# A decoder layer on one core: the spectral stage with one forward transform of the context, exponentials with bias on ScalarE and both products of the weights on GpSimd, one slot deeper

## The reference, cut to what matters

```python
corr = jnp.fft.ifft(qf * jnp.conj(kf), axis=2).real
w, idx = jax.lax.top_k(corr.transpose(0, 1, 3, 2), topk)   # topk = 8
w = jax.nn.softmax(w, axis=-1)
for i in range(topk):
    g = jnp.minimum(idx[:, :, None, :, i] + pos, L - 1)
    out = out + w[:, :, None, :, i] * jnp.take_along_axis(v, g, axis=2)
...
x = x + _L0_xattn_ref(_layernorm(x, axis=-1), ctx_4096, ctx_4096)
x = x + _L0_ffn_ref(_layernorm(x, axis=-1), ...)   # one of 8 adapters per row
```

## Time and profile before

| | |
|---|---|
| three runs | 832.5, 828.73, 832.15 us; median 832.15 |
| profiled execution, first to last instruction | 830.1 us (its own time is not listed apart from this span) |
| TensorE busy | 791.7 us, 95%, 3512 matrix products |
| VectorE, ScalarE, GpSimd busy | 574.7, 406.5, 242.7 us |
| mean granted TensorE clock | 0.987 of full |
| last product of the first stage | ends near 622 us |
| last instruction of VectorE (`dve_final` of tile 15) | starts at 826.91 us |

### The profile page before, as it was taken

One profiled execution on the slowest core, in us unless ns is written; L12 is line 12 of the kernel. 1 busy time (PEld: TensorE's weight loads), 2 busy tenths in 40 slices (PEclk: granted clock), 3 DMA queues, 4 the chain that ended last, 5 costly groups with the idle time before them and its releaser, 6 DMA issues. The chain is left out here.

```text
span 830.1 us, 10669 instructions
## 1 busy us (share of the span) xinstructions
PE 791.7 (95%) x3512; PEld 558.2 (67%) x3512; DVE 574.7 (69%) x1291; ACT 406.5 (49%) x647; POOL 242.7 (29%) x196
## 2 busy tenths in 40 slices
PE   3979999999999999999999999999998999999995
PEld 1335768778788888888888888887764535544542
DVE  5998775576997377386566657723458898888883
ACT  7784753564764454355255344411333445445541
POOL 0001211033453433342343333221213333233231
PEclk9999999999999999999999999999998999999997
DMA  7373210012232022022113102020000101111101
GB/s 215 132 254 126 77 38 1 1 51 69 96 103 90 13 93 85 13 89 76 39 39 97 69 18 72 13 74 1 13 14 13 39 26 51 52 29 49 38 27 39
DMA packets 25655, 50.57 MB, mean 61 GB/s; under 512 B 3264, under 2 KB 3648, under 8 KB 25600
## 3 DMA queue, kind: packets, MB, share of 16 engines
q1 hardware_dynamic: 25600, 49.89, 18.4%
HBM read 45.68 MB, written 4.19 MB: 60 GB/s over the span
## 5 line engine op out<-in xcount | busy, mean ns | idle before, releaser
L673 PE MATMUL ps<-x_hi,w_hi 128*128 128x512 f32 x448 | 176.0, 393 | 0.2 <-POOL w_lo L530 0.2
L675 PE MATMUL ps<-x_hi,w_lo 128*128 128x512 f32 x448 | 174.7, 390 | 0.0
L674 PE MATMUL ps<-x_lo,w_hi 128*128 128x512 f32 x448 | 174.3, 389 | 0.0
L789 POOL TENSOR_TENSOR h_lo<-hf,h_hi 128x512 fp32r<-128x512 f32 x56 | 74.0, 1321 | 243.2 <-ACT h_hi L784 243.2
L798 DVE TENSOR_TENSOR acc<-acc,ps 128x512 f32<-128x512 f32 x112 | 76.5, 685 | 74.9 <-PE ps L675 74.9
L673 PEld LDWEIGHTS ps<-x_hi,w_hi 128*128 128x128 f32 x448 | 84.1, 188 | 21.0 <-issue 3.3
L777 DVE TENSOR_TENSOR hf<-hf,ps 128x512 f32<-128x512 f32 x56 | 38.5, 687 | 85.5 <-PE ps L675 85.5
L675 PEld LDWEIGHTS ps<-x_hi,w_lo 128*128 128x128 f32 x448 | 84.1, 188 | 17.9
L674 PEld LDWEIGHTS ps<-x_lo,w_hi 128*128 128x128 f32 x448 | 84.2, 188 | 17.2
L530 POOL TENSOR_TENSOR w_lo<-wt,w_hi 128x512 fp32r<-128x512 f32 x42 | 62.3, 1484 | 113.8 <-ACT w_hi L523 113.8
L673 PE MATMUL ps<-w_hi,h_hi 128*128 128x512 f32 x224 | 88.2, 394 | 1.5 <-DVE acc L724 1.4
(11 more groups left out here) (151 smaller groups left out, 1381.8 us busy)
## 6 DMA issues: line engine op xcount, KB each, us to landing
codes_sb<-in_codes SPq DMA_DIRECT2D x40, 256.0 KB, 3.1
scale_sb<-in_scale_rows SPq DMA_DIRECT2D x80, 128.0 KB, 2.9
lft<-in_lora_ft SPq DMA_DIRECT2D x14, 512.0 KB, 4.4
acc<-in_x SPq DMA_DIRECT2D x4, 1024.0 KB, 8.5
ctx<-in_ctx SPq DMA_DIRECT2D x16, 256.0 KB, 2.9
out<-fin SPq DMA_DIRECT2D x16, 256.0 KB, 3.1
codes_sb<-in_codes SPq DMA_DIRECT2D x5, 512.0 KB, 3.4
codes_odd<-in_codes SPq DMA_DIRECT2D x4, 512.0 KB, 5.1
```

Of the source, the lines that this page charges most:

```text
L673: nc.tensor.matmul(bank, hi, rhs_hi, start=start, stop=False)
L674: nc.tensor.matmul(bank, hi, rhs_lo, start=False, stop=False)
L675: return nc.tensor.matmul(bank, lo, rhs_hi, start=False, stop=stop)
L789: nc.gpsimd.tensor_tensor(h_lo[:, c % 2, i], hf[:, i], h_hi[:, c % 2, i].bitcast(F32), ALU.subtract).then_inc(hlo_done, 1)
```

## The change

The transforms get other rows: one matrix `KU` holds ordinary and odd frequencies together (real parts in partitions 0 to 63, imaginary parts in 64 to 127, in blocks of 32), so the context is transformed once per tile, and so are the weights (`pe_w` with `WU`). The real and imaginary products then need the same and the crossed halves: `sp_spread` sends the copied spectrum `ku` on by six DMAs inside SBUF, four of 32 partitions into `kc` (for `dve_product`) and two of 64 partitions into `kx`. `dve_cyclic` is gone; GpSimd does both products (`pool_same` with `ku`, `pool_cross` with `kx`). `dve_less` is gone; ScalarE reads the correlation from PSUM in eight ACTIVATEs of 64 columns with the negated maximum `ntop` as bias, and `dve_mark` waits for them. All engines' orders in the slot are new, and a tile takes one slot more from first to last piece.

In the cut diff below, the old order lists and the old forms of functions that the listing above shows are left out.

```diff
-SPEC, KCYC, KNEG, WNEG_M, INV, OUT, OUT_N = range(7)
+SPEC, KU, WU, INV, OUT_S, OUT_X = range(6)
...
+    for k, rows in ((SPEC, (real, imag, real, imag)), (KU, (k_real, neg_real @ less_last, imag, neg_imag @ less_last)),
+                    (WU, (real, neg_real, imag, neg_imag))):
...
+    kc = two("kc", (2, D))
+    kx = sb("kx", [P, KX, 2, D])
...
+    ku = sb("ku", [P, KU_RING, 2, D], at=w1_at)
...
+    BLOCK = slice(0, QB // 2), slice(QB // 2, QB), slice(QB, QB + QB // 2), slice(QB + QB // 2, P)
+    HALVES = slice(0, QB), slice(QB, P)
+    def sp_spread(sp, t, b):
+        r = t % KX
+        sp.wait_ge(ku_copied, t + 1)
+        if real(t - 1):
+            sp.wait_ge(prod, t - 1)
+        for to, of in enumerate((0, 0, 2, 2)):
+            sp.dma_start(kc[BLOCK[to], b], ku[BLOCK[of], t % KU_RING]).then_inc(kc_in[b], 16)
+        if t >= KX:
+            sp.wait_ge(pcross, 2 * (t - KX) + 2)
+        for to in range(2):
+            sp.dma_start(kx[HALVES[to], r], ku[HALVES[1 - to], t % KU_RING]).then_inc(kx_in[r], 16)
...
+    wide = [(FORWARD, 0), (FORWARD, 1), (FORWARD, 2), (FIRST_Q, 0)]
+    for v in range(TT + 5):
+        wide += [(FORWARD, v + 1)] * (3 <= v + 1 < TT) + [(BACKWARD, v - 2)] * (0 <= v - 2 < TT)
+    def wait_for_wide(pe, kind, n):
+        k = wide.index((kind, n))
+        if k > 0:
+            user, m = wide[k - 1]
+            if user == FORWARD:
+                pe.wait_ge(ku_copied, m + 1)
+            elif user == BACKWARD:
+                pe.wait_ge(w_copied, m + 1)
+            else:
+                pe.wait_ge(prod, m + 1)
...
-        elif t > 1:
-            pe.wait_ge(pcyc, t - 1)
+        else:
+            pe.wait_ge(prod, t)
...
-    def pe_kc(pe, t, b, h):
+    def pe_ku(pe, t, b, h):
         pe.wait_ge(ctx_in_s[b], 16 * h + 16)
...
+        wait_for_wide(pe, FORWARD, t)
+        by_sequence(pe, KW, KU, ctx[:, b]).then_inc(ku_ready, 1)
+    def act_ku(act, t):
+        act.wait_ge(ku_ready, t + 1)
+        if t >= KU_RING:
+            n = t - KU_RING
+            act.wait_ge(psame, 2 * n + 2)
+            act.wait_ge(kx_in[n % KX], 32 * (n // KX) + 32)
+        nc.scalar.copy(ku[:, t % KU_RING], pair(KW)).then_inc(ku_copied, 1)
...
-        dve.wait_ge(kc_copied, t + 1)
+        dve.wait_ge(kc_in[b], 64 * (t // 2) + 64)
...
     def dve_top_less(dve, t, b):
         dve.wait_ge(top_done, t + 1)
+        if real(t - 1):
+            dve.wait_ge(exp_done, t - 1)
         nc.vector.tensor_tensor(topd[:, b], top[:, b], top[:, b, :, 0:1].to_broadcast([P, 8, TOPK]),
                                 ALU.subtract).then_inc(topd_done, 1)
...
+        nc.vector.tensor_scalar(ntop[:, b], top[:, b, :, 0], -1.0, None, ALU.mult).then_inc(topd_done, 1)
+    def dve_mark(dve, t, b):
         corr = ps[:, CORR].rearrange("p (r l) -> p r l", l=L)
...
+        dve.wait_ge(exp_done, t + 1)
         if real(t - 1):
             dve.wait_ge(weighed, t - 1)
         for r in range(8):
...
     def act_exp_top(act, t, b):
...
+        act.wait_ge(topd_done, 2 * t + 1)
         flat = topd[:, b].rearrange("p r k -> p (r k)")
         nc.scalar.activation(flat, flat, ACT.Exp).then_inc(top_exp, 1)
     def act_exp(act, t, b):
...
+        corr = ps[:, CORR].rearrange("p (r l) -> p r l", l=L)
+        act.wait_ge(topd_done, 2 * t + 2)
         if real(t - 1):
             act.wait_ge(divided, t - 1)
...
+        for r in range(8):
+            mm = nc.scalar.activation(rows(ex, b)[:, r], corr[:, r], ACT.Exp, bias=ntop[:, b, r:r + 1])
+        mm.then_inc(exp_done, 1)
     def dve_sum(dve, t, b):
         dve.wait_ge(top_exp, t + 1)
...
+    misc = [(LAGS, 0)]
+    for v in range(TT + 5):
+        misc += [(EXPERT, v - 5)] * (0 <= v - 5 < TT) + [(TURN_H, v - 4)] * (0 <= v - 4 < TT) + [(LAGS, v - 2)] * (1 <= v - 2 < TT)
+    def wait_for_misc(pe, kind, n):
+        k = misc.index((kind, n))
+        if k > 0:
+            user, m = misc[k - 1]
+            pe.wait_ge((lag_copied, h_copied, fin_done)[user], m + 1)
...
+    def pe_w(pe, t, b):
         pe.wait_ge(lag_copied, t + 1)
...
+        wait_for_wide(pe, BACKWARD, t)
+        by_sequence(pe, KW, WU, wts[:, b]).then_inc(w_ready, 1)
...
-    def act_negacyclic(act, t, b):
+    def act_w(act, t, b):
...
+            act.wait_ge(psame, 2 * (t - 1))
+            act.wait_ge(pcross, 2 * (t - 1))
+        nc.scalar.copy(wu[:, b], pair(KW)).then_inc(w_copied, 1)
+    def pool_same(pool, t, b):
+        pool.wait_ge(w_copied, t + 1)
         if real(t - 1):
             pool.wait_ge(gathered, t - 1)
         for s in range(2):
...
+            nc.gpsimd.tensor_tensor(pc[:, b, s], wu[:, b, s], ku[:, t % KU_RING, s], ALU.mult).then_inc(psame, 1)
+    def pool_cross(pool, t, b):
+        r = t % KX
+        pool.wait_ge(w_copied, t + 1)
+        pool.wait_ge(kx_in[r], 32 * (t // KX) + 32)
+        if real(t - 1):
+            pool.wait_ge(gathered, t - 1)
+        for s in range(2):
+            nc.gpsimd.tensor_tensor(pn[:, b, s], wu[:, b, s], kx[:, r, s], ALU.mult).then_inc(pcross, 1)
...
-            pe.wait_ge(pcyc, t + 1)
+            pe.wait_ge(psame, 2 * t + 2)
...
-            pe.wait_ge(pneg, 2 * t + 2)
-        mat, src = ((OUT, pc), (OUT_N, pn))[k]
+            pe.wait_ge(pcross, 2 * t + 2)
+        mat, src = ((OUT_S, pc), (OUT_X, pn))[k]
...
             for t in range(2):
                 sp_ctx(sp, t, t)
+            for t in range(3):
+                sp_spread(sp, t, t % 2)
+                sp_ctx(sp, t + 2, t % 2)
             def piece(at):
...
                 if a := at(6):
                     sp_store(sp, *a[:2])
+                if a := at(-1, 3):
+                    sp_spread(sp, *a[:2])
+                if a := at(-3, 5):
+                    sp_ctx(sp, *a[:2])
             slots(sp, piece, 6)
             for b in range(2):
...
             def piece(at):
                 if (a := at(1)) and a[0] in LATER:
                     x_pow(pool, NCH + 2 + a[0] // 4)
...
+                if a := at(3):
+                    pool_same(pool, *a[:2])
+                if a := at(3):
+                    pool_cross(pool, *a[:2])
+                if a := at(1, 1):
                     pool_divide(pool, *a[:2])
...
+                if a := at(3):
                     pool_pow(pool, *a[:2])
...
+            slots(pool, piece, 3)
         @block.scalar
         def _(act):
...
                     for u in units[1:]:
                         act_hi(act, u)
                     act_hhi(act, g, c, 1)
+                    if g == NG - 1 and c == 1:
+                        act_ku(act, 0)
                     if c == 0 and g < NG - 1:
                         act_lft_hi(act, 2 * g + 2 + min(g - 1, 1))
                     elif c == 1 and g == 1:
                         act_lft_hi(act, 2 * g + 3)
                     if g == NG - 1 and c == 2:
...
+                        act_ku(act, 1)
                         for t in range(2):
                             act_normalise_x2(act, t, t)
...
             act_exp_top(act, 0, 0)
             act_exp(act, 0, 0)
...
             act_lags(act, 0, 0)
             def piece(at):
...
+                if a := at(2, 1):
                     act_exp(act, *a[:2])
...
+                if a := at(3):
+                    act_w(act, *a[:2])
                 if a := at(5):
                     act_expert(act, *a[:2])
...
+                if a := at(-1, 3):
+                    act_ku(act, a[0])
                 if a := at(4):
                     act_normalise_x3(act, *a[:2])
+                if a := at(-1, 2):
+                    act_normalise_x2(act, *a[:2])
+                if a := at(4):
+                    act_turn_h(act, *a[:2])
+                if a := at(1, 1):
+                    act_exp_top(act, *a[:2])
+                if a := at(2, 1):
+                    act_lags(act, *a[:2])
             slots(act, piece, 5)
         @block.vector
...
             dve_add(dve, NG - 1, NCH - 1, 3)
             def piece(at):
...
                 if a := at(4):
...
+                    dve_rstd(dve, *a[:2])
                 if (a := at(2)) and a[0] in LATER:
                     x_rstd(dve, NCH + 2 + a[0] // 4)
                 if (a := at(0)) and a[0] in LATER:
                     x_stats(dve, NCH + 2 + a[0] // 4)
+                if a := at(5):
+                    dve_final(dve, *a)
+                if a := at(2, 1):
+                    dve_weigh(dve, *a[:2])
                 if a := at(1, 1):
...
+                    dve_top(dve, *a[:2])
+                if a := at(1, 1):
+                    dve_top_less(dve, *a[:2])
+                if a := at(0, 1):
+                    dve_product(dve, *a[:2])
+                if a := at(1, 1):
+                    dve_sum(dve, *a[:2])
+                if a := at(4):
+                    dve_route(dve, *a[:2])
+                if a := at(3):
                     dve_x3(dve, *a[:2])
                 if a := at(3):
...
                     dve_stats(dve, *a[:2])
...
```

(83 more changed lines are left out.)

153 lines of the change are left out of this document (14 added, 139 removed).

## The result

The changed kernel takes **886.11 us** (median of 4 runs, 885.17 to 887.92) against 832.33 (4 runs, 828.73 to 833.76): a ratio of 1.0656, 95% interval 1.0631 to 1.0681. The forecast was 871, slower, in a range of 815 to 893. The profiled execution has a span of 885.9 us.

The account below looks back on a forecast made before the run. TensorE bounded the old slot at 12.17 us; held dve_rstd would make it 12.7. Sum: 648 + 11 x 12.7 + 3 + 58.9 + 2.5 = 852.1, plus 16.8 for clock, 869; median 871, range 815 to 893.

Parts of the forecast that it names:

- The lock: VectorE's four two-input dve_rstd instructions each wait out a GpSimd product, ending 5.0 us after the products start, not taking 0.64.
- The slot without the clock: VectorE's loop through the held dve_rstd sets a spectral slot of 12.7 us instead of 12.17.
- The clock: TensorE's wait before the norm's transpose lowers its clock: 1.2 us a slot, 16.8 over 14 slots.
- The discount of 0.7: Factor on the 1.65 us clock loss per slot, since not each wait need cost the clock; gave 1.2.
- The eleven slots: Spectral stage from the correlation of tile 3 to that of tile 14: 11 x 12.7 us, plus 3 for later statistics.
- The start: Correlation of tile 3 starts at 648 us, from 643 to 651; before the change it was 648.51.
- The walk: Piece-by-piece pass through the engines' new order; at the start it had TensorE stand 2 to 4 us.
- The end: From the correlation of tile 14 to the last dve_final: 58.9 us, 36 of it to the products of tile 15.
- ScalarE: Eight exponentials of 64 columns at 0.24 us each, 1.9 together, with room on the engine.
- DMA: Six issues and 1 MB inside SBUF per tile, landing in time for dve_product; taken to cost nothing.
- The sum, 869: Whole span: 852.1 us without the clock plus 16.8 for it; the median was put 2 us higher.
- Rival A: The hold doesn't bite, TensorE bounds slots at 10.25 us, and the kernel is faster at 813 us; chance 0.14.

Follow-up runs that it names:

- Experiments 2 and 4: Changed kernel with dve_rstd's four instructions given one tensor input each, 836.4 us; and with GpSimd's products cut to 128 columns, 836.57 us, or joined to 1024, 891.37 us.
- experiment 3: Changed kernel with eight unused small matmuls per slot in TensorE's idle time ahead of the transpose of xh: 863.49 us, ratio 1.038.
- f2_stats_late: Changed kernel with the later tiles' statistics moved from ahead of dve_final to behind the lag marks: 884.58 us, ratio 1.0644.
- e4_start: Changed kernel with the first two additions of the last stage moved ahead of the first lag marks: 884.16 us, ratio 1.0629.
- experiment 2: Changed kernel with the four dve_rstd instructions written as tensor_scalar, one tensor input and a per-partition operand each: 836.4 us, ratio 1.0056.
- the best version: Changed kernel with one-input scale factors, remaining two-input instructions moved, later statistics in pieces, GpSimd products of 256 columns, later power behind them: 824.87 us, ratio 0.9919.
- experiment 1: Changed kernel where GpSimd's products of a tile wait until the four dve_rstd instructions of the tile before are done: 850.64 us, ratio 1.0229.

## Why the prediction was right

Term by term, forecast and trace:

- *The lock.* "`dve_rstd` ends 5.0 us after the products' start instead of taking 0.64": 4.95 (729.08 to 734.03). It starts 0.93 after them (forecast 1.0). Experiments 2 and 4 show the cause.
- *The slot without the clock*, 12.7: experiment 3 has 12.7. PE waits 2.27 in one piece (forecast 2.5).
- *The clock*, 1.2 a slot, 16.8 in all: too small. The quiet slots are 13.97 to 14.22 (one is 13.57), most of them 1.5 over the 12.7, and experiment 3 gives back 22.6. The discount of 0.7 was what failed: the full 1.65 would have been right to within 0.15.
- *The eleven slots* from the correlation of tile 3 to that of tile 14: 162.6 (653.88 to 816.45) against 139.7 + 3 + 13.2 = 155.9, 6.7 over. The clock explains 3.3 (eleven times 0.3). Four of the slots were longer than the rest, by 1.3 to 3.1: the longest holds the later tiles' statistics ahead of `dve_final`.
- *The start*, 648: it was 653.88, 5.9 late. The causes are known in part. The walk had missed that on DVE, at the seam, four statistics (2.5 us) and their aggregates stand ahead of the product of tile 1, for which PE waits 4.87. With them behind it in `f2_stats_late`, the correlation of tile 1 starts at 629.85 instead of 634.94. But it then takes 3.67 instead of 2.58 us, and the correlation of tile 3 is only 1.7 earlier (652.20). The sums behind the marks, which the walk had priced at 2 to 4, are worth 2.0 (`e4_start`), so they are no part of the error. And the correlation of tile 0 was 2.9 later than before already (611.75 to 608.82), of which the forecast had 1.06; over all the versions it lies between 609.3 and 613.0. What makes up the rest stays open.
- *The end*: from the correlation of tile 14 to the end of the last `dve_final` 66.9 against 58.9 and three times 1.2 of clock, 4.4 over. Of this, 3.4 lies between that correlation and the products of tile 15: 43.0 us (816.45 to 859.44), where 36 and three times 1.2 give 39.6. Experiment 3, whose added matmuls run in the drain too, needs 62.2 from the same correlation (797.46 to 859.65) where this kernel needs 66.9. So the clock costs at least 4.7 there and not 3.6; the other 3.3 over the 58.9 stay open, at a granted clock of 0.83 even with the added matmuls (820 to 862 us).
- *ScalarE*: eight exponentials 1.75 (forecast 1.9). *DMA*: `kc` 2.4 us and `kx` 3.6 to landing, and nothing waited for them. `ntop` 0.165 where no product runs. All as forecast.

The sum, 869, was 17 below the span of 886: 5.9 + 6.7 + 4.4. The sign and the mechanism held. All three sizes erred in the same direction, so the errors added up, and 7 us more would have been outside the range.

Rival A priced a kernel without the hold at 813. The nearest run, experiment 2, came to 836, and the best version to 825: removing this hold let others show, and A counted none.

## What to carry to other kernels

Before moving work to GpSimd, list the VectorE instructions that will stand beside it and how many tensors in SBUF each reads. Here each small one in a dependent chain (one column, or four in the earlier trace rows) cost about one GpSimd instruction; the remedies, by their worth here, are one-column forms with a per-partition operand (50 us), shorter GpSimd instructions (50 us), and another place in the order, which helps only if nothing else slides under the product (35 us). When a gap on TensorE is the consequence, price the slower clock behind it too.

## What the hardware showed beyond the forecast

- GpSimd waits too. Where `dve_weigh` starts within a product, the two GpSimd instructions take 2.95 instead of 2.50 (experiment 1). That the second one waits for `dve_weigh` is inferred from the overlap of their times.
- An instruction with one tensor input is held as well if it has eight columns (1.25), and not if it has one (0.21).
- Cutting a GpSimd instruction costs GpSimd time: 128 columns 0.455 (`pc`) and 0.51 (`pn`), 256 columns 0.73 and 0.84, 512 columns 1.25 to 1.28, 1024 columns 2.35, the shorter ones partly beside held DVE instructions. For a tile that is 7.2 us in pieces of 128 and 5.0 in pieces of 512.
- With PE idle for 2.3 us ahead of the transpose in each slot of 14, the granted clock was 0.82 to 0.91 in windows of 20 us; with eight added matmuls in that gap it was 1.00 (700 to 820 us).
